# Vision transformer block in 36-token images: three projected groups ahead of the loop, and dense experts in two batches

## What is computed

```
h = LN(LN(patches)*g1+b1 @ W_proj) * g2 + b2                 # tokens, 192 wide
q, k, v = h @ W_qkv, 8 heads of 24; q, k normalised over the 36 tokens
attn = softmax(q^T k * temp) over 24 x 24;  h = LN(h + (attn v) @ W_o + b_o)
# soft mixture of 8 experts x 4 slots, per image
logits = l2(h) @ l2(slot_params) * scale                      # 36 x 32
Dm = softmax over tokens, C = softmax over slots
X = Dm^T l2(h);  H = gelu(X @ W_down[n] + b_down[n]);  Y = H @ W_up[n] + b_up[n]
out = LN(h + C @ Y)
```

## Time and profile before

| | us |
|---|---|
| runs, median (lowest to highest) | 140.48 (139.16 to 142.77) |
| the profiled execution: its own time | 140.0 |
| the same execution: span from the first to the last instruction | 138.0 |
| PE busy in the span | 115.0 (83%) |
| DVE, ACT, POOL busy | 88.9, 69.0, 67.0 |
| mean granted TensorE clock | 0.939 of full |

### The profile page before, as it was taken

The page is one execution under the profiler, slowest core; times in us unless marked ns, Lnnn a source line. Parts: engine busy times, 40 slices in busy tenths (PEclk is TensorE's granted clock), DMA queues, the critical chain, the costliest instruction groups (busy, mean ns, idle before and its releaser), DMA issues.

```text
span 138.0 us, 4819 instructions
## 1 busy us (share of the span) xinstructions
PE 115.0 (83%) x1779; PEld 93.6 (68%) x1779; DVE 88.9 (64%) x380; ACT 69.0 (50%) x234; POOL 67.0 (49%) x158
## 2 busy tenths in 40 slices
PE   0297799999699999999999999997986860999920
PEld 0297799888377868578787796866964630788700
DVE  0211999999643687985857558586987440159980
ACT  3000004242862848648675686846644468763553
POOL 8500277767847428837265382743664000007871
PEclk9999999999999999999999999999999555599995
DMA  1999899988000000000000000000000000000232
GB/s 14 337 293 278 269 305 320 314 319 214 5 7 0 5 0 7 5 0 7 0 5 5 0 5 0 10 5 0 5 0 7 0 0 0 5 0 24 72 89 71
DMA packets 7677, 10.34 MB, mean 75 GB/s; under 512 B 2056, under 2 KB 5032, under 8 KB 7656
## 3 DMA queue, kind: packets, MB, share of 16 engines
q1 hardware_dynamic: 7656, 10.06, 24.2%
HBM read 9.17 MB, written 0.88 MB: 73 GB/s over the span
## 4 chain that ended last, share of the span: by engine, by line
PE 47%; DVE 22%; issue 12%; POOL 10%; ACT 4%; DMA 3%; SPq 1%; POOLq 1%; DVEq 0%; ACTq 0%
DVE st L649 8%; PE ps L565 7%; PE ps L436 6%; PE ps L476 5%; PE ps L496 3%; PE ps L542 3%; PE ps L399 3%; DMA wt<-in_w_tok 3%; PE ps L489 3%; PE ps L519 3%; DVE y L663 3%; PE ps L578 3%; DVE st L671 2%; PE ps L507 2%; PE ps L407 2%
## 5 line engine op out<-in xcount | busy, mean ns | idle before, releaser
L417 PE MATMUL ps<-wc,xT 128*108 128x192 f32 (+1 forms) x132 | 23.0, 327 | 1.5 <-DVE wc L637 1.5
L940 ACT ACTIVATE hT<-ps,b,g 96x108 f32<-96x108 f32 (+1 forms) x22 | 8.4, 430 | 27.9 <-PE ps L426 27.9
L417 PEld LDWEIGHTS ps<-wc,xT 128*108 128x108 f32 (+1 forms) x132 | 20.7, 170 | 2.0 <-DVE wc L637 1.8
L436 PE MATMUL ps<-wqk,hT 96*108 96x384 f32 (+1 forms) x44 | 16.2, 490 | 0.7 <-ACT qp L962 0.7
L1125 POOL TENSOR_SCALAR pw<-mv 108x1 f32<-108x1 f32 (+1 forms) x11 | 3.7, 337 | 21.3 <-DVE mv L780 21.3
L476 PE MATMUL ps<-hT,wv 96*128 96x108 f32 (+1 forms) x88 | 12.5, 284 | 0.0
L1139 POOL TENSOR_SCALAR var<-mv 108x1 f32<-108x1 f32 (+1 forms) x11 | 2.4, 223 | 18.9 <-DVE mv L875 18.4
L950 ACT ACTIVATE sq<-ps 108x384 f32<-108x384 f32 (+1 forms) x11 | 5.4, 490 | 12.4 <-PE ps L436 12.4
L476 PEld LDWEIGHTS ps<-hT,wv 96*128 96x128 f32 x88 | 10.7, 191 | 0.7
L649 DVE BATCH_NORM_STATS2 st<-xs 108x6 f32<-108x384 f32 (+1 forms) x22 | 10.9, 540 | 0.2 <-issue 0.2
L960 ACT ACTIVATE km<-ps,imgsel 108x192 f32<-108x192 f32 (+1 forms) x32 | 11.0, 418 | 0.0
(11 more groups left out here) (106 smaller groups left out, 304.6 us busy)
## 6 DMA issues: line engine op xcount, KB each, us to landing
xT<-in_x_t SPq DMA_DIRECT2D x10, 324.0 KB, 7.0
xs<-in_x SPq DMA_DIRECT2D x10, 324.0 KB
out<-o SPq DMA_DIRECT2D x10, 81.0 KB
wt<-in_w_tok SPq DMA_DIRECT2D x1, 576.0 KB, 4.2
wqk<-in_w_qk SPq DMA_DIRECT2D x1, 288.0 KB, 8.7
xT<-in_x_t SPq DMA_DIRECT2D x1, 216.0 KB, 7.5
xs<-in_x SPq DMA_DIRECT2D x1, 216.0 KB
wv<-in_w_v SPq DMA_DIRECT2D x1, 192.0 KB, 9.0
```

What stands on the lines that cost most here:

```text
L417: mm = pe.matmul(tokp(g), xT[:, o + kc * n:o + (kc + 1) * n], wc[:, kc, :], start=kc == 0, stop=kc == KC - 1)
L436: mm = pe.matmul(qkp(g), hT[:, f, t0:t0 + tokens(g)], wqk[:, f, :, :, :].rearrange("p j h d -> p (j h d)"), start=f == 0, stop=f == 1)
L940: ins = act.activation(hT[:, f, t0:t0 + tokens(g)], htp(g)[:, f, :], ACT.Identity, bias=b2[:, f:f + 1], scale=g2[:, f:f + 1])
```

## The change

**In front.** The gain and the bias of the first layer norm come in one DMA, `W_proj` in two halves whose rows are contiguous. `column_means` takes the raw weights as soon as they land, with the gain over 768 (`gs1`, one small DVE instruction) as the stationary operand; before, it waited for scaled weights `wg`. DVE writes `wc` in six fused instructions and PE's `token(0)` starts behind the first. `offset` moves behind `token(0)`. DVE takes `bw` (`token_offset`) after the statistics of group 0. Memsets for `share`, `wu` and `hb` go.

**The projection.** P1 is 3. `TOKENS` puts the groups 3 to 10 into the steps 0 to 5: two in each of steps 0 and 1, one in each of 2 to 5. Their transposes stand two steps later. DVE and POOL have the matching calls in their steps. `load_x(4)` and later are issued behind the slots' DMAs.

**The experts.** Two batches, groups 0 to 4 and 5 to 10. `hidden(b)` writes all 32 rows of an expert's padded block; `gelu(b)` takes a batch in two instructions over 128 rows. `widen(b)` (new, PE, 16 products of 32 rows) makes each expert's output for a whole batch, transposed; `take_lower` (ACT) and `take_upper` (DVE) copy it out, and `turn_u(g)` (PE, two transposes) brings a group's 96 slots to rows; `take_y(g)` (ACT) copies these. `combine(g)` is two accumulating products, the first with `bu` in place of DVE's `slot_bias`. `WIDE` puts `turn_u` of the groups 0, (1, 2), 3, 4 into the steps 13 to 16 and their `combine` one step later; `hidden(0)` stands at the head of PE's step 11, `gelu(0)` in ACT's step 11 behind `take_c`, `widen(0)` at the end of step 12. The second batch follows the loop.

```diff
-HB = ((0, 4), (4, 8), (8, NG))
+HB = ((0, 5), (5, NG))
+NBI = 17
+HS = 11
+WIDE = {13: (0,), 14: (1, 2), 15: (3,), 16: (4,)}
...
-P1 = 9
+P1 = 3
+TOKENS = {0: (3, 4), 1: (5, 6), 2: (7,), 3: (8,), 4: (9,), 5: (10,)}
...
-            sp.dma_start(g1[:, :], ln1_g).then_inc(ln1_in, 16)
-            sp.dma_start(b1[:, :], ln1_b).then_inc(ln1_in, 16)
-            sp.dma_start(wt[:, :, :], w_tok.rearrange("(k p) e -> p k e", p=128)).then_inc(wtok_in, 16)
+            sp.dma_start(gb1[:, :, :].rearrange("p t k -> p (t k)"), ln1_gb).then_inc(ln1_in, 16)
+            for i in range(2):
+                k0 = i * KC // 2
+                sp.dma_start(wt[:, k0:k0 + KC // 2, :].rearrange("p k e -> p (k e)"),
...
+            def column_means():
+                pe.wait_ge(gs1_ready, 1)
+                for kc in range(KC):
+                    if kc % (KC // 2) == 0:
+                        pe.wait_ge(wtok_in[kc // (KC // 2)], 16)
+                    mm = pe.matmul(csp(), gs1[:, kc:kc + 1].broadcast_to([128, 128]), wt[:, kc, :],
+                                   start=kc == 0, stop=kc == KC - 1)
+                mm.then_inc(csp_ready, 1)
             def offset():
...
-                i0, i1 = HB[b][0] * GI, min(B, HB[b][1] * GI)
+                i0, i1 = batch(b)
                 pe.wait_ge(xt_ready, HB[b][1])
...
                 for n in range(NE):
-                    j = n % 4
+                    j = n // 2
                     for f in range(2):
-                        mm = pe.matmul(hp(b, i1 - i0)[32 * j:32 * j + HID, n // 4, :, :], wd[:, f, n, :],
+                        mm = pe.matmul(hp(b, i1 - i0)[32 * j:32 * j + 32, n % 2, :], wd[:, f, n, :],
                                        xt[:, f, i0:i1, n, :], start=f == 0, stop=f == 1,
                                        tile_position=(0, 32 * j))
                 mm.then_inc(hp_ready, 1)
 
-            def slot_out(g):
-                i0, ni = g * GI, images(g)
-                pe.wait_ge(hb_ready, 1 + sum(g >= e for _, e in HB[:-1]))
+            def widen(b):
+                i0, i1 = batch(b)
+                pe.wait_ge(hb_ready, b + 1)
...
+                for e in range(2):
+                    for f in range(2):
+                        for j in range(4):
+                            r = slice(32 * j, 32 * j + 32)
+                            mm = pe.matmul(utp(i1 - i0)[:, j, f, :, e, :], wu[r, e, f * F:(f + 1) * F],
+                                           hb[r, e, 0:(i1 - i0) * NP], start=True, stop=True,
+                                           tile_position=(32 * j, 0))
+                mm.then_inc(utp_ready, 1)
+            def turn_u(g):
+                b = sum(g >= e for _, e in HB[:-1])
+                i0 = (g - HB[b][0]) * GI
...
-                for e in range(2):
-                    mm = pe.matmul(ytp(g), hb[:, e, i0:i0 + ni, :, :].rearrange("p i n q -> p (i n q)"),
-                                   wu[:, e, :], start=e == 0, stop=e == 1)
+                for f in range(2):
+                    u = widened(b)[:, f, i0:i0 + images(g), :, :]
+                    mm = pe.transpose(ytp(g)[:, f * F:(f + 1) * F],
+                                      u.rearrange("p i j s -> p (i j s)"), ident[0:F, 0:F])
                 mm.then_inc(ytp_ready, 1)
 
             def combine(g):
-                pe.wait_ge(yt_ready, g + 1)
+                n, sl = tokens(g), images(g) * SL
                 pe.wait_ge(cT_ready, g + 1)
...
-                pe.matmul(yop(g), cT[0:images(g) * SL, g, 0:tokens(g)], yt[0:images(g) * SL, g % NQ, :],
-                          start=True, stop=True).then_inc(yop_ready, 1)
-
-            offset()
+                pe.matmul(yop(g), cT[0:sl, g, 0:n], bu[0:sl, :], start=True, stop=False)
+                pe.wait_ge(yt_ready, g + 1)
+                pe.matmul(yop(g), cT[0:sl, g, 0:n], yt[0:sl, g % NQ, :], start=False, stop=True).then_inc(yop_ready, 1)
             column_means()
-            pe.wait_ge(wc_ready, 1)
             for g in range(P1):
                 token(g)
+                if g == 0:
+                    offset()
                 if g == 2:
                     pe.wait_ge(ident_in, 16)
                 if g >= 2:
...
+                if s == HS:
+                    pe.wait_ge(experts_in, 16 * (3 + 1))
+                    hidden(0)
                 at(values, s - 2)
                 at(project, s - 3)
...
-                at(turn_h, s + P1 - 2 - 1, P1 - 2)
-                at(token, s + P1 - 1, P1)
+                if s < P1 - 1:
+                    turn_h(s + 1)
+                late(turn_h, s - 2, 0)
+                late(token, s, 0)
                 at(gram, s - 1)
                 at(mix, s - 2)
+                late(turn_h, s - 2, 1)
                 at(turn_xn, s - 4)
                 at(slot_in, s - 6)
                 at(norms, s)
-                if s == NG + 2:
-                    pe.wait_ge(experts_in, 16 * (3 + 4))
-                    pe.wait_ge(qk_ready, NG)
-                    hidden(0)
-                if s == NG + 3:
-                    pe.wait_ge(v_ready, NG)
-                    hidden(1)
-            pe.wait_ge(lnn_ready, NG)
-            pe.wait_ge(e2_scaled, NG)
-            slot_out(0)
-            slot_out(1)
-            hidden(2)
-            for g in range(2, NG):
-                slot_out(g)
-                combine(g - 2)
-            combine(NG - 2)
+                late(token, s, 1)
+                if s == HS + 1:
+                    widen(0)
+                for g in wide(s - 1):
+                    combine(g)
+                for g in wide(s):
+                    turn_u(g)
+            combine(4)
+            hidden(1)
+            widen(1)
+            turn_u(5)
+            for g in range(6, NG):
+                turn_u(g)
+                combine(g - 1)
             combine(NG - 1)
...
+            def mean_shares():
+                dve.wait_ge(ln1_in, 16)
+                dve.tensor_scalar(gs1[:, :], gb1[:, 0, :], 1.0 / PD, None, ALU.mult).then_inc(gs1_ready, 1)
             def token_weights():
-                dve.wait_ge(ln1_in, 32)
-                dve.wait_ge(wtok_in, 16)
+                dve.wait_ge(csp_ready, 1)
                 for kc in range(KC):
-                    dve.tensor_scalar(wg[:, kc, :], wt[:, kc, :], g1[:, kc:kc + 1], None,
-                                      ALU.mult).then_inc(wg_ready, 1)
-                dve.wait_ge(wg_ready, KC)
-                dve.wait_ge(csp_ready, 1)
-                dve.tensor_tensor(wc[:, :, :], wg[:, :, :], csp().unsqueeze(1).broadcast_to([128, KC, D]),
-                                  ALU.subtract).then_inc(wc_ready, 1)
+                    dve.scalar_tensor_tensor(wc[:, kc, :], wt[:, kc, :], gb1[:, 0, kc:kc + 1], csp(),
+                                             ALU.mult, ALU.subtract).then_inc(wc_ready, 1)
...
+            def take_upper(b):
+                i0, i1 = batch(b)
+                dve.wait_ge(utp_ready, b + 1)
+                if b >= 1:
+                    dve.wait_ge(ytp_ready, HB[b][0])
+                dve.tensor_copy(widened(b)[:, :, :, 2:4, :].rearrange("p f i j s -> p j (f i) s"),
+                                utp(i1 - i0)[:, 2:4, :, :, :, :].rearrange("p j f i e q -> p j (f i) (e q)")).then_inc(uT_upper, 1)
...
+            mean_shares()
             token_weights()
             x_stats(0)
             x_moments(0)
+            token_offset()
             for s in range(P1):
                 at(x_stats, s + 1)
                 at(x_moments, s + 1)
...
+                if s == HS + 1:
+                    take_upper(0)
+                for g in wide(s - 1):
+                    last_residual(g)
+                for g in wide(s - 1):
+                    last_stats(g)
+                    last_moments(g)
+                for g in wide(s - 2):
+                    last_shift(g)
+            take_upper(1)
+            last_shift(4)
+            for g in range(5, NG + 1):
+                at(last_residual, g, 5)
+                at(last_stats, g, 5)
+                at(last_moments, g, 5)
+                at(last_shift, g - 1, 5)
...
             def gelu(b):
-                i0, i1 = HB[b][0] * GI, min(B, HB[b][1] * GI)
+                i0, i1 = batch(b)
                 act.wait_ge(hp_ready, b + 1)
-                for n in range(NE):
-                    r = slice(32 * (n % 4), 32 * (n % 4) + HID)
-                    ins = act.activation(hb[r, n // 4, i0:i1, n, :], hp(b, i1 - i0)[r, n // 4, :, :],
-                                         ACT.Gelu, bias=bd[r, n // 4:n // 4 + 1])
+                if b >= 1:
+                    act.wait_ge(utp_ready, b)
+                for e in range(2):
+                    ins = act.activation(hb[:, e, 0:(i1 - i0) * NP], hp(b, i1 - i0)[:, e, :],
+                                         ACT.Gelu, bias=bd[:, e:e + 1])
                 ins.then_inc(hb_ready, 1)
...
+                if s == HS:
+                    act.wait_ge(experts_in, 16 * (3 + 1))
```

(23 more changed lines are left out.)

201 lines of the change are left out of this document (118 added, 83 removed).

## The result

The changed kernel takes 157.3 us (four executions, 155.4 to 159.6), the kernel before 141.9 us beside it: the ratio is 1.118 (1.105 to 1.132). A first measurement gave 1.122 (1.110 to 1.133). The prediction of 142.3 us, range 136.3 to 147.0, was wrong. Executions of one kernel differ here in how long PE stays at the lower of its two levels, so ratios compare the faster executions of both kernels, and can differ from the quotient of the medians, and single times are given with their mean granted clock where that matters.

What follows compares the result with a forecast made beforehand. Bounds: DVE and PE share the front, PE the loop to step 10, latency from step 11. Span 92.1 + 45.9 = 138.0 us, time 140.0 at full clock; 2.3 for the lower clock gives 142.3, range 136.3 to 147.0.

Steps and rivals of the forecast that it cites:

- T: End of step 10 on PE: at 92.1 us against 93.08 before, a gain of 1.0 us; bounds 91.3 to 94.0.
- predicted, full clock: Whole kernel with the full clock throughout: span 92.1 + 45.9 = 138.0 us, time 140.0 us.
- The waits and the chain: Step 11 to the end: waits and serial chain put the end at T+45.9 us against T+44.9 before.
- the sum: Added stage times: bw at 14.6, T at 92.1, end at T+45.9; with 2.3 for the clock, 142.3 us.
- The detour on ACT: Step 11, between cT and eC: table load, two gelus and load back, 3.2 us; lm of group 7 delayed 4.6.
- going by the row: ACT's table loads: 1.28 us each without a drain, as profiled; by the skill page the time would be 2.7 us longer.
- The clock: Lower level (1.2 GHz) from step 12 until steps 14 and 15: PE pieces in steps 12 to 14 add 2.3 us.
- Rival 4: Lower level stays from step 12 into the second batch, combine and turn_u 2.1 us a group: 146.8 us, chance 0.25.
- `bw`: Front, the projection's offset on DVE: ready at 14.6 us (13.8 to 16.5), against 14.44 before.
- hide behind that, and cost nothing unless a group lands over 5 us late: Projection: DMAs of later groups and smaller memsets hidden behind PE's steps 2 to 5, 6.9 to 7.6 us with 2.12 more.
- the pace of the second batch: The end: residuals follow at DVE's 1.1 us a group; nearer than 1 or beyond 1.5 us would be wrong.
- Rival 3: Step 11: gelu's detour hidden, logits of group 7 only 1.75 us late, clock stays up: 136.8 us, chance 0.18.

Runs made afterwards that it cites:

- e8: The change with extra 192-column products on PE wherever it waited in the tail: 141.2 us, 0.990 of the kernel before.
- e2: The change with the projection placed as before, nine groups in front of the loop: 156.9 us, ratio 1.109 to the kernel before.
- e5: The change with three extra 192-column products on PE in the wait ahead of hidden(0): 155.5 us.
- e10: The change without the bias product of combine: 150.9 us against the change's 157.3.
- e3: The kernel before with only the projection's place moved, three groups in front: 140.0 us, ratio 1.005.
- e12: e8 with the weights prepared as in the kernel before: 141.4 us over ten executions, 139.3 to 149.0.
- e13: e3 with extra products on PE in the waits of its own tail: 135.6 us, 0.964 of the kernel before.
- e11: e3 with gelu(0) ahead of copies of groups 9 and 10, and slot_out(0), slot_out(1) moved earlier on PE: 141.2 us, ratio 1.008.
- e18: e8 with the experts of hidden issued as 0, 2, 4, 6, 1, 3, 5, 7: 143.9 us.
- e7: The kernel before with hidden(0), for groups 0 to 4, at the head of step 11: executions of 140.5, 148.2, 149.8 and 151.7 us.
- e16: The change with ten extra 192-column products and an added wait for xnT at the head of PE's step 12: 160.9 us.
- e9: The kernel before with the change's weight preparation alone: 144.8 us against 141.0, ratio 1.021.
- e17: The kernel before with only w_tok's transfer changed, to two transfers with rows of 2304 bytes: 143.9 us against 140.5.

## Why the prediction was wrong, step by step

The distances from T, the end of step 10, in us:

| step | predicted, full clock | e8, clock 1.00 | the change, 0.54 |
|---|---|---|---|
| T itself | 92.1 | 95.4 | 95.7 |
| `hidden(0)` starts (wait) | 1.8 | 1.8 (filled) | 1.8 |
| `logits(7)` | 10.1 | 10.5 | 13.2 |
| `turn_dc(10)` | 25.6 | 24.9 | 33.9 |
| `slot_in(10)` ends | 27.0 | 26.5 | 35.6 |
| first residual, batch 2 | 35.1 | 34.5 | 45.1 |
| last residual | 40.7 | 39.7 | 53.1 |
| end | 45.9 | 44.5 | 57.9 |

**The waits and the chain: right.** With the clock held behind T, every step of the tail came within 1.4 us of the sum, and the change itself has the 1.81 us wait. The detour on ACT was 3.1 us for 3.2, and a table load 1.28 us with the gelu 0.01 us behind it, as ACT's timeline of the change shows:

```profile
103.56 0.26 ACT L1103 ACTIVATE cT<-ps 96x108 f32<-96x108 f32 x1 [2.40 <-DVE dm L918]
103.84 1.28 ACT L1117 ACT_TABLE_LOAD   x1
105.13 0.51 ACT L1117 ACTIVATE hb<-ps,bd 128x60 f32<-128x60 f32 x2
105.66 1.28 ACT L1090 ACT_TABLE_LOAD   x1
106.96 0.37 ACT L1090 ACTIVATE eC<-lm,mC 108x96 f32<-108x96 f32 x1
```

The drain that the Trainium skill (ScalarE: Activation LUTs, What ACT_TABLE_LOAD costs) adds behind a load did not appear; going by the row was right.

**The clock: the step that failed.** I wrote that the lower level would hold "from step 12, until steps 14 and 15, which the added products make dense", and priced it at 2.3 us. The change shows it from the head of step 11 almost to the end, and it costs 57.9 - 44.5 = 13.4 us of span, 16 us of median time. Most of this is its length, not its early start: e2 and e5, in which it fell only at 108 and 106 us, and then, but for a short return, stayed low to the end, still took 56.2 us from T. Two readings were at fault. I took PE's long hole to be between T+8 and T+12.8 and overlooked that the wait of 1.8 us, which I had found myself, follows the last norms of step 10: the window around it has 1.59 of 3.40 us busy, less than the one of the earlier trace rows in front of the fall. And I took the return of the level in the earlier trace rows, at the end of one window of 3.40 of 3.40, for what a busy PE brings about; here it stood at 0.50 through window after window of 3.39 and 3.40. Busy time at the lower level is work stretched to up to double its length (`values(9)`, 2.05 for 1.14), and in these windows it did not foretell a return. This second reading is the one that carried the sum: it let the low level end in steps 14 and 15 and left the second batch at full speed. Rival 4 named the mechanism for the second batch, with 6.8 us in place of 16.

**T: the second failure.** T was 3.6 us late, and this has three parts. `bw` came at 15.43, within its bounds but 0.8 us behind the 14.6 of the sum. Then PE waited. The front in the change, PE and ACT:

```profile
9.19 4.15 PE L458 MATMUL ps<-wc,xT 128*108 128x192 f32 x12 [0.60 <-DVE wc L705]
...
20.72 0.77 ACT L1030 ACTIVATE hT<-ps,b,g 96x108 f32<-96x108 f32 x2 [18.71 <-PE ps L469]
22.77 1.99 PE L479 MATMUL ps<-wqk,hT 96*108 96x384 f32 x4 [2.15 <-DMA negmask<-const_negmask]
...
24.91 3.19 PE L458 MATMUL ps<-wc,xT 128*108 128x192 f32 x12
```

And the piece of the chain of waits that released it (start, us, what):

```profile
10.55 11.26 DMA negmask<-const_negmask
```

The loop's first product stands behind the mask, which landed 11.3 us after its issue, before 9.2. The prediction had the DMAs "hide behind that, and cost nothing unless a group lands over 5 us late"; it had no term for this one. Of the wait of 2.15 us the mask accounts for 1.1 here: ACT had the transposed group ready at 21.49, and in e5, where the mask was in time, `qk(0)` followed 0.2 us behind that point. In other traces with the change's transfers it was more; in e10 the group was ready at 20.33 and `qk(0)` started at 24.07.

The third part, 1.6 us, is the clock again. The windows behind this wait in the change:

```profile
20.40:23.80 3.40, 1.25 (x5) 0.61 (x4) 2.25 (x7) 0.77 (x2) 2.24 (x6) 0.98 1.02 270
23.80:27.20 3.40, 3.40 (x12) 2.75 (x11) 1.41 (x4) 2.28 (x7) 0.04 (x1) 0.52 0.85 224
```

The level fell behind PE's wait, and the next `token` took 3.19 us instead of 2.12. The other traces bear this out: in the eight in which PE waited 2.15 to 4.61 us for the mask, the clock line is low somewhere between 18 and 30 us, and in the four in which it waited only 1.0 us in this place (e3, e5, e12, e13), it is full there. From `qk(0)` to T PE was busy 71.8 of 72.9 us; in e12, without such a stretch, 70.2 of 71.3. The arithmetic itself was right where neither a late mask nor the level came in: e12 and e13, with the old transfers, have `qk(0)` at 20.75 and 20.52 and T at 92.0. The old transfers are no guarantee, since e11 waited 2.33 us for the mask with them, and e5, with the new ones, a mask in time and the level full, still took 72.8 us from `qk(0)` to T, with two short waits more (0.58 and 0.54 us). e8 has the mask's wait too, 2.90 us, and the low stretch behind it, so that its T, 95.4, is as late as the change's.

**Sizes.** `hidden(0)` was put at 0.6 us and took 1.3 (e18 shows why); the pace of the second batch, 1.1, is 1.04 at the full level and 1.59 at the low one, beyond the 1.5 named as a sign of being wrong. Rival 3 is out: in e8 `logits(7)` still waited for ACT's xnT and stood at T+10.5.

So 138.0 predicted at the full clock, + 3.6 for T, + 12.0 for the tail, gives the change's 153.6 us of span.

## What to carry to other kernels

When a change puts a wait in front of PE, price the whole stretch behind it at both levels, not the wait: 1.85 us cost 0.4 us in one execution of e7 and 8 to 11 us in three others. Read the granted clock next to the busy share, because at the lower level PE looks like the bound and is it. In such a stretch less work helps (e10, 6.4 us), and work in the waits ahead of it helped more (e8, 16 us). Don't count on a full PE to bring the level back. And keep a cheap filler product at hand as an experiment: it tells whether a slow tail is slow by its structure or by its clock, and where it stands in a wait anyway it can stay in the kernel (e13, 3.6% faster).

## What the runs showed of the hardware

- Products that follow one another in the same 32-column tile took twice as long as the same products going round the tiles: 1.33 and 0.67 us for 32 instructions of 60 columns, at the full level.
- With work removed from PE the program became longer: 0.7 us less in `hidden(0)`, 2.7 us more in all, at a lower clock (e18 against e8).
- The level came back to full behind windows in which PE was busy for 3.36 to 3.40 of 3.40 us in e16 and e10, and stayed at 0.50 through several of the same kind in the change. A PE wait of 2.15 to 4.61 us in front of `qk(0)` had a low stretch at it or behind it in all eight traces that have one, a wait of 1.0 us in the same place in none of four; the added wait of 3.06 us in e16 had a fall within it. A wait of 1.8 us in front of `hidden(0)` had one right behind it in the change, and not in e2 and in the profiled execution of e7.
- A transfer of 576 KB with rows of 2304 instead of 768 bytes went with more packet time for the whole load: 38.0 and 38.3 us for 10.06 MB in e9 and e17, 36.0 to 40.2 over all eleven traces with it, 33.4 to 37.8 over the eight without. No run here says by what.
